# A graph layer on one core: in each step the transposes of the probabilities go behind the score matmul and the projections

## The chip, the cores and the metric

The kernel runs on one core of a Trainium2 chip. The metric is the device time of one execution in microseconds (us). TensorE is called PE here, VectorE DVE, ScalarE ACT, GpSimd POOL and SyncE SP. SP only issues transfers. Each engine executes its own instruction stream in the order in which it is written, and engines wait for each other through semaphores.

## What is computed

The input is 16 graphs of 512 nodes with 512 features each, and a 512x512 adjacency matrix for each graph. Two layers follow each other, each with a residual and a layer norm:

```
q, k, v = heads(x @ Wq.T), heads(x @ Wk.T), heads(x @ Wv.T)      # 16 heads of 32
a = einsum('bhnd,bhmd->bhnm', q, k) * scale + (adj + adj)
a = where(any(a != 0, axis=-1), a, -inf);  p = where(isnan(softmax(a)), 0, softmax(a))
x = layernorm(x + (p @ v, heads joined) @ Wo.T)
top1 = argmax(x.mean(axis=1) @ router_w + router_b);  W = expert_w[top1]     # one of 4
out = adj @ (x @ W);  mean, var = statistics of out over all graphs of the same expert
x = layernorm(x + relu((out - mean) * rsqrt(var + eps) * gamma + beta))
```

## The kernel before, in words

**Steps.** Attention is cut into steps. A step is one head and one tile of 128 query rows. Four heads are a group and are worked on together. A unit `u` is one group and one row tile, so it has 4 steps (`HG = 4`). A graph has 16 units and 64 steps, and 16 graphs give 1024 steps. A step handles a 128x512 tile of scores.

**One tile's way through the engines.** PE multiplies q and k into a PSUM bank (`pe_scores`, L325). There are two score banks. DVE adds the adjacency and finds the row extreme (`dve_logits`, L468). POOL folds the tile to a row sum that tells whether a row is all zero (L617, L619, L624). ACT takes the exponential (`act_exp_step`, L407). DVE normalises (L494). PE transposes the tile with four 128x128 transposes into one of two banks, `t_bank` (`pe_turn`, L334). ACT copies this bank to `pt` (L446). After two units PE multiplies `pt` with v (`pe_pv`, L347): 32 matmuls, once per 8 steps. This is called the PV block below, and there are 8 per graph.

**A software pipeline.** In step r the engines work on different tiles: PE transposes tile r and makes the scores of tile r + 12 (`LEAD = 12`). ACT copies the transposed tile r and takes the exponential of tile r + 10 (`EXP_LEAD = 10`). DVE does the logits of tile r + 12 and the normalisation of tile r + 6.

**Projections as filler.** All dense matmuls of the two layers are tasks: "V", "K", "Q" make v, k, q of this graph, and "Q+", "K+" those of the next. "O-", "sum-", "route-", "X-", "S-", "M-" finish the graph before: output projection, column means, router, transposes of x, x times expert, adjacency product. A task has four chunks, and most chunks are three 128x512 matmuls (L252 to L254), since each float32 operand is split into a high and a low part. A fixed list (`TASKS`, `HALF_SLOTS`) spreads the chunks over the 64 steps: in most steps one or two. Tasks alternate between two banks, `p_bank`. The first chunk of a task waits until the earlier task on its bank has been read out.

**Who reads a task out.** ACT and DVE have their part of a task in the step in which its last chunk stands. ACT does it behind the copy to `pt` and behind the exponential of that step. For Q, K, X and S tasks ACT copies the high part, and then DVE subtracts it to form the low part (L500, L501). For V and M tasks ACT reads alone, for O tasks DVE reads alone. These places matter here:

- V, task 3 has its last chunk in step 7, the step before the first PV block of a graph. The PV block also waits for v to be complete (`act_v`).
- X tasks 0 and 1 stand in step 32, and K+ task 0 begins in step 33 on the bank of X task 0.
- S task 0 ends in step 37, and S task 1 begins in step 38 with data from X task 1, on the bank that K and S tasks used; its predecessor there is S task 0.
- S task 1 ends in step 40, and S task 2 begins in step 41 on the same bank.
- In steps 24 to 27 ACT splits the next graph's transposed input, one quarter each step, ahead of that step's copy to `pt`. DVE makes the low part. Q+ task 0 in step 28 waits for all quarters.

**ACT's order in a step** (`act_slot`): wait for the transposes of tile r, copy them to `pt`, exponential of tile r + 10, then the tasks of the step. **DVE's order** (`dve_slot`): logits of tile r + 12, normalisation, then the tasks of the step.

**PV's waits** are these lines of `pe_pv`; the first asks for the copies of all transposes up to the end of the unit:

```
wait(eng, act_pt, b, STEPS, 4 * u + 4)
wait(eng, dve_ot, b, PAIRS, pair - 1)
wait(eng, act_v, b, NT, NT)
```

The first graph has no work of a graph before it (no O-, sum-, route-, X-, S-, M- tasks). The last has no Q+ and K+ tasks. The 14 graphs between have all tasks. Behind the 16 graphs one more round finishes the last graph without any attention steps, and a final loop normalises all graphs (from L1007 on DVE).

Of the kernel before, what the change touches and what calls it, by code (L numbers as in the profile page):

```python
# [54 lines left out]
def build_gnn_layers(nc, x, xT, adj, adjT, wqT, wkT, wvT, woT, router_w, router_b, experts, gammaT, betaT, out):  # L55
# [16 lines left out]
    with ctx:  # L72
# [89 lines left out]
        def wait(eng, s, b, per, more):  # L162

            if isinstance(b, int):
                if per * b + more > 0:
                    eng.wait_ge(s, per * b + more)
            else:
                assert per * 2 + more > 0
                eng.wait_ge(s, b * per + more)
                if eng.engine == mybir.EngineType.SP:  # L170
                    settle(eng)
# [59 lines left out]
        def wait_bank(eng, b, task, kind, kind_before):  # L231
            t, back = bank_user_before(task, kind, kind_before)
            s, per, more = done_by(b, t)
            wait(eng, s, b, per, more - per * back)
# [10 lines left out]
        def plan(u, kind):  # L245

            return [[c for c in step_chunks[HG * u + j] if present(c[0][0], *kind)] for j in range(HG)]


        def three_pass(eng, bank, lhs, rhs, kt, last):  # L250

            eng.matmul(bank, lhs(0), rhs(0), start=(kt == 0), stop=False)  # L252
            eng.matmul(bank, lhs(0), rhs(1), start=False, stop=False)  # L253
            return eng.matmul(bank, lhs(1), rhs(0), start=False, stop=last)  # L254

        def pe_chunk(eng, b, task, c, kind, kind_before):

            name, i = task
            bank = p_bank[bank_of[task]]
            if c == 0:  # L260
                wait_bank(eng, b, task, kind, kind_before)
            if name[0] in "QK":
                which = "QK".index(name[0])
                g = i if not name.endswith("+") else GROUPS + i
                if c == 0:
                    first = sum(t[0] == ("Q+", "K+")[which] for t in AHEAD)
                    wait(eng, (ld_qw, ld_kw)[which], b, GROUPS * 16, (g + 1 - first) * 16)
                    if i == 0:
                        wait(eng, dve_xt, b, DT, 2 * DT)
                        wait(eng, act_xt, b, DT, 2 * DT)  # L270
                mm = three_pass(eng, bank[:, :], lambda h: qk_w[:, which, h, c, :], lambda h: xt[:, h, c, :],
                                c, c == DT - 1)
            elif name == "V":
                if c == 0 and i == 0:
                    wait(eng, ld_wv, b, 16, 16)
                mm = three_pass(eng, bank[:, :], lambda h: xt[:, h, c, i * P:(i + 1) * P],
                                lambda h: slot_a[:, h, c, :], c, c == DT - 1)
            elif name == "O-":
                if c == 0 and i == 0:
                    wait(eng, ld_wo, b, 16, 0)  # L280
                    wait(eng, dve_ot, b, PAIRS, 0)
                mm = three_pass(eng, bank[:, :], lambda h: ot[:, h, c, i * P:(i + 1) * P],
                                lambda h: slot_b[:, h, c, :], c, c == DT - 1)
            elif name == "sum-":
                if c == 0:
                    wait(eng, dve_x1, b, NT, 0)
                for t in range(NT):
                    mm = eng.matmul(bank[:, c:c + 1], x1[:, t, c * P:(c + 1) * P], ones[:, :],  # L288
                                    start=(t == 0), stop=(t == NT - 1))
            elif name == "route-":  # L290
                if c == 0:
                    wait(eng, dve_mean, b, 1, 0)
                mm = eng.matmul(bank[:, 0:E], xmean[:, c:c + 1].to_broadcast([P, P]), rw[:, c, :],
                                start=(c == 0), stop=(c == DT - 1))
            elif name == "X-":
                mm = eng.transpose(bank[:, c * P:(c + 1) * P], x1[:, i, c * P:(c + 1) * P], ident[:, :])
            elif name == "S-":
                if c == 0:
                    wait(eng, dve_lo["X"], b, NT, i + 1 - NT)
                    if i == 0:  # L300
                        wait(eng, ld_ex, b, 16, 0)
                mm = three_pass(eng, bank[:, :], lambda h: x1t[:, i % 2, h, c, :], lambda h: slot_a[:, h, c, :],
                                c, c == DT - 1)
            else:
                if c == 0 and i == 0:
                    wait(eng, dve_lo["S"], b, NT, 0)
                    wait(eng, pool_at, b, NT, 0)
                mm = three_pass(eng, bank[:, :], lambda h: sup[:, h, c, i * P:(i + 1) * P],
                                lambda h: slot_b[:, h, c, :], c, c == NT - 1)
            if c == 3:  # L310
                mm.then_inc(pe[name.rstrip("+-")], 1)
# [5 lines left out]
        def pe_scores(eng, b, r):  # L317

            u, j = divmod(r, HG)
            g, t = divmod(u, NT)  # L320
            if j == 0 and t == 0:
                wait_stacked(eng, 0, b, g)
                wait_stacked(eng, 1, b, g)
            wait(eng, dve_logit, b, STEPS, r - 1)
            eng.matmul(s_bank[r % 2][:, :], q_stack[:, g % 2, j, t * P:(t + 1) * P], k_stack[:, g % 2, j, :],  # L325
                       start=True, stop=True).then_inc(pe["score"], 1)

        def pe_turn(eng, b, r):

            u, j = divmod(r, HG)  # L330
            wait(eng, dve_norm, b, STEPS, r + 1)
            wait(eng, act_pt, b, STEPS, r - 1)
            for m in range(NT):
                mm = eng.transpose(t_bank[r % 2][:, m * P:(m + 1) * P],  # L334
                                   att[:, u % 4, j, m * P:(m + 1) * P], ident[:, :])
            mm.then_inc(pe["turn"], 1)

        def pe_pv(eng, b, u):

            pair, g = u // 2, u // NT  # L340
# [3 lines that stand above are left out]
            for m in range(NT):  # L344
                for j in range(HG):
                    head = g * HG + j
                    mm = eng.matmul(o_bank[pair % 2][j * HD:(j + 1) * HD, 0:2 * P],  # L347
                                    v[:, m, head * HD:(head + 1) * HD], pt[:, j, m, :],
                                    start=(m == 0), stop=(m == NT - 1), tile_position=(0, j * HD))
            mm.then_inc(pe["pv"], 1)  # L350

        def pe_slot(eng, b, u, kind, kind_before):
            attends, has_next = kind[2], kind[1]
            work = plan(u, kind) if u >= 0 else [[]] * HG
            for j in range(HG):
                r = HG * u + j
                if attends and r >= 0:
                    pe_turn(eng, b, r)
                if (attends and r + LEAD < STEPS) or (has_next and r + LEAD >= STEPS):
                    pe_scores(eng, b, r + LEAD)  # L360
                for task, c in work[j]:
                    pe_chunk(eng, b, task, c, kind, kind_before)
            if attends and u >= 0 and u % 2 == 1:
                pe_pv(eng, b, u)

# [712 lines left out]
```

## Time and profile before

| | |
|---|---|
| time, median of 3 runs | 2675.96 us (2672.56 to 2677.76) |
| profiled execution: its own time | 2680.46 us |
| span in the profile | 2678.7 us |
| PE busy | 2336.3 us, 87% |
| DVE busy | 2075.9 us, 77% |
| ACT busy | 1715.0 us, 64% |
| POOL busy | 1784.4 us, 67% |
| mean granted clock of PE | 0.904 of full speed |

The times are of unprofiled runs. The profile is of one separate execution. Busy time of PE is modelled: matmuls overlap, so that a start-to-start distance is shorter than the printed duration (three 128x512 matmuls start 0.23 us apart and are printed with 0.39 us each).

### The profile page before, as it was taken

What the parts mean: (1) busy time and instruction counts of PE and PEld (TensorE: products, weight loads), DVE (VectorE), ACT (ScalarE), POOL (GpSimd) and SP (SyncE); (2) the same over time, 40 slices, a digit from 0 to 9 for tenths busy, and PEclk for the clock granted to TensorE, in tenths of its full rate; (3) what the DMA queues carried; (4) which work ended last, traced back from release to release, by engine and by line L of the source; (5) the groups of instructions that cost most, each with busy time, mean ns of one, the idle gap of its engine ahead of it and who ended that gap; (6) DMA issues with size and microseconds to landing.
All of it is one profiled execution on the core that took longest, in us unless ns stands there. A gap on an engine that the chain in (4) does not pass through costs nothing.

```text
span 2678.7 us, 50494 instructions
## 1 busy us (share of the span) xinstructions
PE 2336.3 (87%) x14976; PEld 1826.5 (68%) x14976; DVE 2075.9 (77%) x5107; ACT 1715.0 (64%) x3838; POOL 1784.4 (67%) x3148
## 2 busy tenths in 40 slices
PE   2678999999999999999999999999999999986433
PEld 2456777777777777777777777777777777765332
DVE  2687878887887878788888878787887887872588
ACT  0467676777767676767677676777776776762232
POOL 0678786877777777868777777777786877770000
PEclk7789898999989898989999898989998999987755
DMA  6577464555555565646555555656464555523597
GB/s 213 185 233 228 147 216 147 172 175 159 173 176 177 153 204 149 214 143 190 158 162 173 177 177 154 204 154 205 151 212 136 173 167 175 148 81 122 189 332 248
DMA packets 215897, 478.88 MB, mean 179 GB/s; under 512 B 41424, under 2 KB 49616, under 8 KB 208720
## 3 DMA queue, kind: packets, MB, share of 16 engines
q1 hardware_dynamic: 215632, 475.71, 56.7%
q8 instruction: 121, 1.98, 0.3%
q14 instruction: 144, 1.18, 0.1%
HBM read 274.23 MB, written 67.11 MB: 127 GB/s over the span
## 4 chain that ended last, share of the span: by engine, by line
PE 68%; DVE 13%; ACT 5%; issue 5%; POOL 4%; SPq 3%; DMA 2%; DVEq 0%; POOLq 0%; ACTq 0%
PE t_bank L334 14%; PE p_bank L252 12%; PE p_bank L254 11%; PE p_bank L253 11%; PE o_bank L347 9%; PE s_bank L325 7%; PE p_bank L288 3%; SPq L646 2%; DVE att L468 2%; ACT att L407 2%; POOL fold L617 2%; DVE ln_raw L1004 2%; DVE att L494 1%; POOL fold L619 1%; DVE xt L500 1%
## 5 line engine op out<-in xcount | busy, mean ns | idle before, releaser
L617 POOL TENSOR_TENSOR fold<-att 128x256 f32<-128x256 f32 x1024 | 821.3, 802 | 471.3 <-DVE nmax L468 366.9
L446 ACT ACTIVATE pt<-t_bank 128x512 f32<-128x512 f32 x1024 | 611.5, 597 | 561.1 <-PE t_bank L334 550.1
L468 DVE CUSTOM_DVE_ANT_0 att<-s_bank,adj_t 128x512 f32<-128x512 f32 x1024 | 699.0, 683 | 297.2 <-PE s_bank L325 295.4
L407 ACT ACTIVATE att<-att,nmax 128x512 f32<-128x512 f32 x1024 | 736.0, 719 | 85.5 <-POOL fold L617 63.2
L494 DVE TENSOR_SCALAR att<-att,small 128x512 f32<-128x512 f32 x1024 | 689.1, 673 | 9.3
L334 PE MATMUL t_bank<-ident,att 128*128 128x128 f32 x4096 | 644.4, 281 | 6.5 <-ACT pt L446 6.3
L334 PEld LDWEIGHTS t_bank<-ident,att 128*128 128x128 f32 x4096 | 515.7, 145 | 186.4 <-issue 48.5
L619 POOL TENSOR_TENSOR fold<-fold 128x128 f32<-128x128 f32 x1024 | 523.2, 511 | 80.3
L325 PE MATMUL s_bank<-k_stack,q_stack 128*128 128x512 f32 x1024 | 504.2, 493 | 80.4 <-DVE nmax L468 80.0
L624 POOL TENSOR_TENSOR fold<-fold 128x64 f32<-128x64 f32 x1024 | 357.9, 349 | 80.2
L347 PE MATMUL o_bank<-pt,v 128*32 128x256 f32 x4096 | 276.1, 415 | 28.0 <-ACT pt L446 15.6
L325 PEld LDWEIGHTS s_bank<-k_stack,q_stack 128*128 128x128 f32 x1024 | 201.3, 197 | 93.5 <-DVE nmax L468 90.9
L252 PE MATMUL p_bank<-xt,qk_w 128*128 128x512 f32 x492 | 207.4, 422 | 35.0 <-DVE xt L500 23.8
L347 PEld LDWEIGHTS o_bank<-pt,v 128*32 128x32 f32 x4096 | 130.6, 117 | 147.7 <-issue 50.7
L254 PE MATMUL p_bank<-xt,qk_w 128*128 128x512 f32 x492 | 204.5, 416 | 0.0
L253 PE MATMUL p_bank<-xt,qk_w 128*128 128x512 f32 x492 | 204.1, 415 | 0.0
L407 ACT ACTIVATION_READ_ACCUMULATOR att<-att,nmax 128x1 f32 x1024 | 198.2, 194 | 0.0
L252 PEld LDWEIGHTS p_bank<-xt,qk_w 128*128 128x128 f32 x492 | 101.0, 205 | 52.7 <-issue 28.4
L252 PE MATMUL p_bank<-slot_a,x1t 128*128 128x512 f32 x256 | 104.3, 408 | 29.3 <-DVE sup L500 21.1
L476 DVE TENSOR_REDUCE small<-fold 128x4 f32<-128x256 f32 x256 | 106.3, 415 | 27.5 <-POOL fold L624 26.8
L376 ACT ACTIVATE qk_t<-p_bank 128x512 fp32r<-128x512 f32 x128 | 75.7, 591 | 76.7 <-DMA q_stack<-qk_t 37.0
L631 POOL TENSOR_TENSOR slot_b<-stage,slot_b 128x512 fp32r<-128x512 f32 x64 | 83.6, 1327 | 55.8 <-ACT slot_b L431 55.8
(150 smaller groups left out, 3591.5 us busy)
## 6 DMA issues: line engine op xcount, KB each, us to landing
q_stack<-qk_t SPq DMA_DIRECT2D x1024, 64.0 KB, 2.0
k_stack<-qk_t SPq DMA_DIRECT2D x1024, 64.0 KB, 2.0
qk_w<-qk_split SPq DMA_DIRECT2D x123, 512.0 KB, 4.3
slot_a<-vo_split SPq DMA_DIRECT2D x16, 2048.0 KB, 8.2
slot_b<-vo_split SPq DMA_DIRECT2D x16, 2048.0 KB, 9.5
slot_a<-expert_split SPq DMA_DIRECT2D x16, 2048.0 KB, 8.1
stage<-in_xT SPq DMA_DIRECT2D x16, 1024.0 KB, 14.9
adj_t<-in_adj SPq DMA_DIRECT2D x64, 256.0 KB, 3.1
```

Source lines behind the costliest of these rows:

```text
L252: eng.matmul(bank, lhs(0), rhs(0), start=(kt == 0), stop=False)
L253: eng.matmul(bank, lhs(0), rhs(1), start=False, stop=False)
L254: return eng.matmul(bank, lhs(1), rhs(0), start=False, stop=last)
L325: eng.matmul(s_bank[r % 2][:, :], q_stack[:, g % 2, j, t * P:(t + 1) * P], k_stack[:, g % 2, j, :], start=True, stop=True).then_inc(pe["sc ...
L334: mm = eng.transpose(t_bank[r % 2][:, m * P:(m + 1) * P], att[:, u % 4, j, m * P:(m + 1) * P], ident[:, :])
L347: mm = eng.matmul(o_bank[pair % 2][j * HD:(j + 1) * HD, 0:2 * P], v[:, m, head * HD:(head + 1) * HD], pt[:, j, m, :], start=(m == 0), stop ...
L407: eng.activation(att[:, u % 4, j, :], att[:, u % 4, j, :], ACT.Exp, bias=nmax[:, u % 4, j:j + 1], scale=-1.0, accum_out=rsum[:, u % 4, j:j ...
L446: eng.activation(pt[:, j, :, (u % 2) * P:(u % 2 + 1) * P], t_bank[r % 2][:, :].rearrange("p (m n) -> p m n", m=NT), ACT.Copy).then_inc(act ...
L468: eng.tensor_tensor_reduce(out=att[:, u % 4, j, :], in0=s_bank[r % 2][:, :], in1=adj_t[:, t, :], scale=-2.0, scalar=3.0e38, op0=ALU.add, o ...
L494: eng.tensor_scalar(att[:, u % 4, j, :], att[:, u % 4, j, :], rinv[:, j:j + 1], live[:, j:j + 1], ALU.mult, ALU.mult).then_inc(dve_norm, 1)
L617: eng.tensor_tensor(fold1[:, :], a[:, 0:256], a[:, 256:512], ALU.add).then_inc(pool_fold1, 1)
L619: eng.tensor_tensor(fold1[:, 0:P], fold1[:, 0:P], fold1[:, P:2 * P], ALU.add).then_inc(pool_halved, 1)
```

## The change

In each step of `pe_slot` the call of `pe_turn` moves from the front to the end, behind the score matmul and behind the step's chunks. The PV block, which follows every eighth step, stays where it is, and so comes directly behind the transposes. Nothing else is changed: the same instructions with the same waits are issued, and the other engines keep their order.

```diff
             for j in range(HG):
                 r = HG * u + j
-                if attends and r >= 0:
-                    pe_turn(eng, b, r)
                 if (attends and r + LEAD < STEPS) or (has_next and r + LEAD >= STEPS):
                     pe_scores(eng, b, r + LEAD)
                 for task, c in work[j]:
                     pe_chunk(eng, b, task, c, kind, kind_before)
+                if attends and r >= 0:
+                    pe_turn(eng, b, r)
             if attends and u >= 0 and u % 2 == 1:
                 pe_pv(eng, b, u)
```

## Rows read from the trace of the kernel before

**Rows 1.** The page: busy time by engine, and the chain by engine.
```profile
PE 2336.3 (87%) x14976; PEld 1826.5 (68%) x14976; DVE 2075.9 (77%) x5107; ACT 1715.0 (64%) x3838; POOL 1784.4 (67%) x3148
...
PE 68%; DVE 13%; ACT 5%; issue 5%; POOL 4%; SPq 3%; DMA 2%; DVEq 0%; POOLq 0%; ACTq 0%
```

**Rows 2.** Waits, whole span: who waits for whom, us in total, times, longest.
```profile
ACT pt L446 <- PE t_bank L334: 550.1, 492, 6.9
...
DVE att L468 <- PE s_bank L325: 295.4, 248, 3.8
...
PE s_bank L325 <- DVE nmax L468: 80.0, 35, 29.2
```

**Rows 3.** Windows: one graph in the middle; us, busy by engine, clock.
```profile
1137.00:1287.00 150.00, 143.57 (x946) 112.60 (x939) 120.63 (x302) 105.51 (x239) 112.43 (x198) 0.94 0.56 170
```

**Rows 4.** Timeline before a graph's first PV block: start, us, engine, work, [idle before].
```profile
1132.33 0.60 PE L334 MATMUL t_bank<-ident,att 128*128 128x128 f32 x4
...
1132.96 0.60 ACT L446 ACTIVATE pt<-t_bank 128x512 f32<-128x512 f32 x1 [0.71 <-PE t_bank L334]
...
1133.45 0.71 ACT L407 ACTIVATE att<-att,nmax 128x512 f32<-128x512 f32 x1
...
1134.59 0.60 ACT L382 ACTIVATE v<-p_bank 128x512 f32<-128x512 f32 x1 [0.33 <-PE p_bank L254]
1135.33 1.93 PE L347 MATMUL o_bank<-pt,v 128*32 128x256 f32 x32 [0.78 <-ACT v L382]
```

**Rows 5.** Timeline at an ordinary PV block, step 15.
```profile
1149.55 0.60 PE L334 MATMUL t_bank<-ident,att 128*128 128x128 f32 x4
...
1150.68 0.40 PE L254 MATMUL p_bank<-slot_b,ot 128*128 128x512 f32 x1
...
1151.01 1.93 PE L347 MATMUL o_bank<-pt,v 128*32 128x256 f32 x32
```

**Rows 6.** Timeline in the first graph, whose steps are short.
```profile
128.80 3.35 PE L347 MATMUL o_bank<-pt,v 128*32 128x256 f32 x32 [2.66 <-ACT pt L446]
```

**Rows 7.** Timeline, steps 32 and 33: X transposes, exponential, first K+ chunk.
```profile
1197.92 1.04 PE L296 MATMUL p_bank<-ident,x 128*128 128x128 f32 x8
...
1198.99 0.19 ACT L407 ACTIVATION_READ_ACCUMULATOR att<-att,nmax 128x1 f32 x1
...
1200.45 0.50 PE L252 MATMUL p_bank<-xt,qk_w 128*128 128x512 f32 x1 [0.83 <-DVE x1t L500]
```

**Rows 8.** Timeline, steps 37 and 38: from S task 0 to S task 1.
```profile
1208.82 0.60 PE L334 MATMUL t_bank<-ident,att 128*128 128x128 f32 x4
...
1210.31 0.68 DVE L500 TENSOR_TENSOR sup<-p_bank,sup 128x512 fp32r<-128x512 f32 x1
...
1211.04 0.50 PE L252 MATMUL p_bank<-slot_a,x1t 128*128 128x512 f32 x1 [0.95 <-DVE sup L500]
```

**Rows 9.** Timeline, steps 40 and 41: from S task 1 to S task 2.
```profile
1217.28 0.60 PE L334 MATMUL t_bank<-ident,att 128*128 128x128 f32 x4
1217.48 0.60 ACT L394 ACTIVATE sup<-p_bank 128x512 fp32r<-128x512 f32 x1 [0.32 <-PE p_bank L254]
...
1218.85 0.50 PE L252 MATMUL p_bank<-slot_a,x1t 128*128 128x512 f32 x1 [0.31 <-DVE sup L500]
```

**Rows 10.** Timeline, steps 25 to 28: the split of the next input.
```profile
1170.67 0.60 PE L334 MATMUL t_bank<-ident,att 128*128 128x128 f32 x4
...
1172.73 0.60 PE L334 MATMUL t_bank<-ident,att 128*128 128x128 f32 x4
...
1173.37 0.60 ACT L446 ACTIVATE pt<-t_bank 128x512 f32<-128x512 f32 x1 [0.24 <-PE t_bank L334]
...
1176.18 0.61 ACT L440 ACTIVATE xt<-stage 128x512 fp32r<-128x512 f32 x1
...
1177.26 0.94 DVE L500 TENSOR_TENSOR xt<-stage,xt 128x512 fp32r<-128x512 f32 x1
...
1178.46 0.76 PE L252 MATMUL p_bank<-xt,qk_w 128*128 128x512 f32 x1 [1.65 <-DVE xt L500]
```

**Rows 11.** Windows behind these waits; the column after POOL is the granted clock.
```profile
1177.00:1184.00 7.00, 5.54 (x15) 4.48 (x16) 6.96 (x16) 5.13 (x11) 5.00 (x10) 0.51 0.41 103
...
1199.00:1202.00 3.00, 2.17 (x12) 1.53 (x11) 2.58 (x7) 3.00 (x9) 1.97 (x4) 1.00 0.93 399
```

## The prediction, written before the changed kernel was run

> **What bounds the kernel now.** I read the page first. PE is busy 87% of the span, and the chain of work that ended last runs on PE for 68% and on DVE for 13% [rows 1]. Then the list of waits. The two largest are ACT waiting for the transposes, 550.1 us in 492 waits, and DVE waiting for scores, 295.4 us; the other way round PE waited for DVE's logits for only 80.0 us, of which one wait was 29.2 us [rows 2]. So PE sets the pace and the others wait for it. Third, the windows: a graph in the middle takes 150 us and PE is busy for 143.57 us of them [rows 3]. A microsecond that PE loses inside a graph is therefore lost for good, unless it falls where PE waits for ACT or DVE anyway. Such places are few: the waits of rows 4 and 7 to 10.
>
> **What the change does to PE's stream.** Transposes T, scores S and chunks C come in the order T S C T S C before, and S C T S C T after. In the middle of a run of steps this is the same cycle; the transposes are only one place later with regard to the scores. Nothing is added or removed, no transfer or queue is touched. The normalised tile that T reads was made six steps earlier, so T has nothing new to wait for. S finds its bank as free as before. The steps between two events cost nothing. What changes is what T's position sets off: ACT starts its step with a wait for T, and so everything that ACT does in a step, the task read-outs too, moves from beside S and C to behind them.
>
> **Part 1: ordinary PV blocks.** PV needs the copy of the transposes of its last step. Before, S and C lie between T and PV. At step 15, T starts at 1149.55, the last chunk matmul at 1150.68, and PV at 1151.01 without a wait [rows 5]. After, PV is next behind T. From T's start to ACT's copy is 0.63 us (1132.33 to 1132.96), the copy takes 0.60, and a read-out on ACT ends 0.14 us before PV starts (1134.59 + 0.60 to 1135.33) [rows 4]: together 1.37 us. Chunk end to PV was 0.10 us (a third matmul is done 0.23 after its start: 1150.91 to 1151.01). So PV comes 1.27 us later behind the last chunk, less the 0.36 us of T that no longer stand ahead of that chunk: +0.91 us. Seven of the eight PV blocks of a graph are of this kind: 6.4 us. The lower end is 0, if ACT's copy were hidden; nothing stands between T and PV to hide it. The upper end is the 2.66 us that PV waited for the same copy in the first graph, where a step holds little but T and S [rows 6]. I take 0.91, since its pieces are all from a full graph.
>
> **Part 2: the first PV block of a graph.** It also needs V task 3, whose read-out stands on ACT behind copy and exponential. The row has 0.95 us from V's last chunk (1134.38) to PV. After, it is 0.63 + 0.49 (copy start to exponential start) + 0.90 (exponential with its accumulator read) + 0.60 + 0.14 = 2.76 us [rows 4], so +1.81 less 0.36: +1.45 us.
>
> **Part 3: tasks that wait for the task just before.** Here ACT's high part and DVE's low part of one task stand between two chunks. After the change, from the last chunk's end: 0.63 + 0.49 + 0.90 on ACT behind T, 0.60 high part, about 0.70 low part, 0.14 to PE = 3.46 us. Before:
> - S task 0 to S task 1: 1208.82 to 1211.04 = 2.22 us, with a PE wait of 0.95 [rows 8]. +1.24.
> - S task 1 to S task 2: 1217.28 to 1218.85 = 1.57 us, because ACT was free at once (1217.48) [rows 9]. +1.89.
> - X to K+: 2.53 us from the first X transpose (1197.92) to K+ [rows 7]. After: 0.88 for the eight X transposes, then 3.46, less the 0.68 of T32 (at half clock) that no longer stands ahead: 3.66. +1.1.
>
> The sum is 4.2 us per graph. The lower end is 0, where DVE and not the read-out was late; the upper end is the full 3.46 thrice, 10.4. PE's own work in between is in both numbers. I stay at 4.2: in two of the three the idle time of PE is put down to just this low part.
>
> **Part 4: the split of the next input, steps 25 to 28.** ACT is a chain of its own here. Its copy of tile 25 now waits for a T that starts at 1172.37 instead of 1170.67 (behind the chunks), 1.70 later. Of that, ACT's own idle 0.24 goes, and DVE's low part began 0.47 after the high part was ready (1176.18 + 0.61 to 1177.26): +1.0 us left on Q+ [rows 10]. Bounds: 0 and 1.7.
>
> **Part 5: DVE held by the late high parts.** DVE stands still until ACT has written the high part of its task, now up to 3.4 us after the task's last chunk; logits of the next tile are queued behind that low part. They end some 4.15 us after the chunk. The score matmul that needs this bank comes three steps later, 3.8 us after the chunk if the two steps are of 1.37 and 2.06 us, 4.5 if both are long. Short by 0.45 or not at all. For 12 such tasks a graph the bounds are 0 and 5.4 us. I take 2.0, since some of the 12 are in Part 3 already or have a PV block behind them.
>
> **Sum.** 6.4 + 1.45 + 4.2 + 1.0 + 2.0 = 15.0 us for each of 14 full graphs: 210. The last graph has no parts 4 and 5: 12. The first has few tasks and its PV blocks wait already: 3. Together 225 us, no gain anywhere to set against it, except that S follows PV directly (below). The profiled execution took 2680.5 us, span 2678.7: 2905 after. The median of the runs is 4.5 us lower: 2901.
>
> **Rivals.**
> - *Only the PV blocks count* (22%). DVE is busy 120.63 of 150 us [rows 3], and a PE that stands at PV lets DVE and ACT catch up, so that parts 3 to 5 hit engines with more slack. For: DVE's work trails its scores in the busy stretches. Against: the S waits are set by latency, not by a backlog. Then 15 x 7.9 = 118, and 2794.
> - *The clock falls at the new waits* (20%). PE's two waits of 1.57 and 1.65 us before Q+ are followed by 7 us at a granted clock of 0.51 [rows 10, 11], that is the lower of the two levels, 1.2 GHz. Waits of 0.62 and 0.83 us near 1200 left it at 1.00 [rows 7, 11]. New waits of some 2.2 us at V, K+ and S lie between these. If two of them per graph start such a stretch, each costs half of 7 us: 14 x 2 x 3.4 = 95, and 2996. The Trainium skill, in "TensorE: Matmul & The Clock Gate", Part 4, says that transposes don't count as PE activity in the way of matmuls; the change puts them right ahead of the waits, and by that page this rival is likelier than I make it. The trace neither shows it nor excludes it: there transposes run at a granted clock of 1.00, but always between matmuls.
> - *Scores behind PV decide, and it gets faster* (4%). During a PV block DVE runs out of scores (its waits for them are 295.4 us [rows 2]). The change lets S follow PV without T between, 0.41 us sooner, 128 times: 52 us, and 2624. This would decide if DVE's logits were what the end hangs on. Against: PE waited for them only 80 us, DVE catches up within a step, and the price of part 1 is paid ahead of each of these gains.
> - *Nothing moves* (4%). The cycle is the same, and waits swap places: within 0.2% of 2676. It needs PE slack of 1 us at each PV block, which rows 5 don't show.
>
> **From these to the numbers.** The forecast has 50%: 2901. The range reaches from just under the PV-only case to just over the clock case, 2785 to 3005. About 0.2% is what a measurement of this kernel can tell from no change. Faster 0.04, same 0.04, slower 0.92.
>
> **What would show it.** In the changed profile the wait of PE's `o_bank` for ACT's `pt` grows from a few us to about 7 x 0.95 us a graph, 100 us or more in the whole, each close to 1 us. The first PV of a graph waits 2 us or more for v. The waits of PE for S and X low parts become 2 us each. The time from one graph to the next grows from 150 to some 165 us, and PE's share falls to about 80%. The waits of DVE and POOL for PE grow. If the wait at PV is missing, or the graph's period is still near 150 us, part 1 is wrong. If a period is above 170 us and the granted clock below 0.88, the clock rival holds. If PE waits for logits (L468) after Q and K tasks, part 5 is larger than I took it.

## The result and the profile after

The changed kernel takes 2937.68 us (median of 4 runs, 2935.32 to 2939.50) against 2674.26 for the kernel before beside it: ratio 1.0983, 95% interval 1.0964 to 1.1002. That is 263 us more. I had forecast 2901 (225 more) within 2785 to 3005, and slower with 0.92. The direction and the range held, and so did the mechanism of the two largest terms; the size was 37 us short.

The page of the changed kernel. The first line answers to the busy times in [rows 1], the second to the chain there:

```profile
PE 2399.5 (82%) x14976; PEld 1854.9 (63%) x14976; DVE 2058.0 (70%) x5107; ACT 1695.4 (58%) x3838; POOL 1785.6 (61%) x3148
...
PE 59%; DVE 17%; ACT 10%; issue 7%; POOL 2%; SPq 2%; DMA 1%; DVEq 0%; ACTq 0%; POOLq 0%
```

The counts of instructions are those of before, so no engine has more to do. PE's busy time is still 63 us longer; some of its matmuls are printed longer at half clock, as shown below. Its busy share falls from 87% to 82%, while the share of ACT and DVE in the chain grows by 9 points. This is how added latency looks, as against added work.

The waits of the changed kernel, whole span, with the columns of [rows 2]:

```profile
ACT pt L446 <- PE t_bank L334: 956.7, 684, 6.0
...
PE s_bank L325 <- DVE nmax L468: 120.2, 75, 29.1
...
PE o_bank L347 <- ACT pt L446: 83.4, 112, 2.2
...
PE p_bank L252 <- DVE sup L500: 63.5, 33, 2.2
...
PE p_bank L252 <- DVE x1t L500: 33.1, 14, 2.4
...
PE o_bank L347 <- ACT v L382: 31.4, 16, 2.0
...
PE p_bank L293 <- DVE small L524: 14.4, 16, 1.6
```

The same waits of the kernel before, as far as [rows 2] does not have them:

```profile
PE p_bank L252 <- DVE sup L500: 22.5, 33, 1.5
...
PE o_bank L347 <- ACT pt L446: 15.6, 10, 2.9
PE o_bank L347 <- ACT v L382: 12.5, 16, 0.8
...
PE p_bank L252 <- DVE x1t L500: 11.2, 14, 0.8
...
PE p_bank L293 <- DVE small L524: 6.3, 16, 0.8
```

The number of waits is the thing to see. PV waited for the copy 10 times, now 112 times: every ordinary PV block of all 16 graphs, 7 x 16. The low-part waits are as many as before (33 and 14) and nearly three times as long in total.

**The time from one graph to the next** is read from the first PV block of two graphs in a row, on PE's timeline. In the kernel before, the block after that of [rows 4] (1135.33) starts at 1282.10, so a graph takes 146.8 us:

```profile
1282.10 1.93 PE L347 MATMUL o_bank<-pt,v 128*32 128x256 f32 x32 [0.78 <-ACT v L382]
```

After, the first PV row below to the second is 164.1 us. Over 14 graphs the means are 146.5 and 163.8 us, 17.3 us apart. The row above the first is that of the transposes right ahead of it.

```profile
1240.12 0.60 PE L334 MATMUL t_bank<-ident,att 128*128 128x128 f32 x4
...
1242.68 1.93 PE L347 MATMUL o_bank<-pt,v 128*32 128x256 f32 x32 [1.97 <-ACT v L382]
...
1406.76 1.94 PE L347 MATMUL o_bank<-pt,v 128*32 128x256 f32 x32 [1.96 <-ACT v L382]
```

**An ordinary PV block after**, step 15, which answers to [rows 5]:

```profile
1258.30 0.60 PE L334 MATMUL t_bank<-ident,att 128*128 128x128 f32 x4
...
1258.93 0.60 ACT L446 ACTIVATE pt<-t_bank 128x512 f32<-128x512 f32 x1 [0.41 <-PE t_bank L334]
...
1259.58 1.93 PE L347 MATMUL o_bank<-pt,v 128*32 128x256 f32 x32 [0.69 <-ACT pt L446]
```

From the transposes' start to PV it is 1.28 us, of which the transposes issue for 0.36. So PE stands still for 0.92 us. The row says 0.69, because PE's ends are modelled: the transposes are printed with 0.60 us. A wait behind transposes is 0.24 us longer than its row. A wait behind a chunk is longer than its row too, by 0.17 us, since the last matmul is printed with 0.40 and takes 0.23. Before, 0.10 us lay between chunk and PV [rows 5], so the change adds 0.82 us.

**The waits for low parts after**, which answer to [rows 7, 8, 9]:

```profile
1313.60 0.79 PE L252 MATMUL p_bank<-xt,qk_w 128*128 128x512 f32 x1 [2.36 <-DVE x1t L500]
...
1326.75 0.56 PE L252 MATMUL p_bank<-slot_a,x1t 128*128 128x512 f32 x1 [2.03 <-DVE sup L500]
...
1338.60 0.50 PE L252 MATMUL p_bank<-slot_a,x1t 128*128 128x512 f32 x1 [1.93 <-DVE sup L500]
```

Before they were 0.83, 0.95 and 0.31 us. The first of these matmuls is printed with 0.79 us against 0.50 in [rows 7]: PE's granted clock has just fallen. The windows show it; the third number from the right is the granted clock, 0.5 of full speed being 1.2 GHz:

```profile
1310.00:1313.00 3.00, 1.24 (x10) 0.92 (x8) 0.63 (x4) 1.96 (x5) 1.74 (x3) 1.00 0.64 273
1313.00:1317.00 4.00, 3.40 (x11) 2.71 (x11) 3.25 (x8) 1.10 (x3) 1.57 (x3) 0.57 0.00 0
1322.00:1326.00 4.00, 2.73 (x16) 2.06 (x14) 3.56 (x8) 3.65 (x9) 3.84 (x5) 1.00 0.42 101
1326.00:1330.00 4.00, 3.25 (x10) 2.69 (x11) 2.41 (x8) 0.95 (x2) 3.35 (x7) 0.63 0.45 109
```

The kernel before has no half-clock stretch in these two places. Its granted clock was 0.904 over 2678.7 us, the changed kernel's 0.897 over 2937.7: 257 us and 303 us of full clock withheld (span times the missing share), 45 us more.

**Steps 25 to 28 after**, which answer to [rows 10]:

```profile
1283.96 0.50 PE L325 MATMUL s_bank<-k_stack,q_stack 128*128 128x512 f32 x1 [0.54 <-DVE nmax L468]
...
1287.97 0.80 PE L325 MATMUL s_bank<-k_stack,q_stack 128*128 128x512 f32 x1 [3.08 <-DVE nmax L468]
1290.12 0.76 PE L252 MATMUL p_bank<-xt,qk_w 128*128 128x512 f32 x1 [1.36 <-DVE xt L500]
```

DVE makes the low part of the input ahead of its logits, and it stood still 2.36 us for ACT's high part:

```profile
1282.58 0.71 DVE L500 TENSOR_TENSOR xt<-stage,xt 128x512 fp32r<-128x512 f32 x1 [2.36 <-ACT xt L440]
```

PE stands still for 0.54 + 3.08 + 1.36 = 4.98 us. Before, it waited 1.65 us for xt [rows 10] and once for logits, which this row of the kernel before shows; together 3.22:

```profile
1176.31 0.50 PE L325 MATMUL s_bank<-k_stack,q_stack 128*128 128x512 f32 x1 [1.57 <-DVE nmax L468]
```

### The profile page after: what moved, and what is told of

Read it like the earlier page. It is cut to its first block, busy times and chain, and to the rows that moved or that the text cites. A ratio compares the mean times of both kernels' runs of the same rounds, so it can differ in the third digit from the quotient of the medians.

```text
span 2937.7 us, 50494 instructions
## 1 busy us (share of the span) xinstructions
PE 2399.5 (82%) x14976; PEld 1854.9 (63%) x14976; DVE 2058.0 (70%) x5107; ACT 1695.4 (58%) x3838; POOL 1785.6 (61%) x3148
## 4 chain that ended last, share of the span: by engine, by line
PE 59%; DVE 17%; ACT 10%; issue 7%; POOL 2%; SPq 2%; DMA 1%; DVEq 0%; ACTq 0%; POOLq 0%
PE t_bank L334 11%; PE p_bank L252 10%; PE p_bank L254 10%; PE p_bank L253 10%; PE o_bank L347 9%; PE s_bank L325 7%; ACT att L407 4%; DVE att L468 4%; ACT pt L446 3%; DVE att L494 3%; DVE ln_raw L1004 2%; PE p_bank L288 1%; SPq L646 1%; POOL fold L617 1%; DVE ln_raw L518 1%
## 5 line engine op out<-in xcount | busy, mean ns | idle before, releaser
L407 ACT ACTIVATE att<-att,nmax 128x512 f32<-128x512 f32 x1024 | 734.1, 717 | 20.9 <-POOL fold L617 17.3
L494 DVE TENSOR_SCALAR att<-att,small 128x512 f32<-128x512 f32 x1024 | 666.9, 652 | 9.3
L334 PEld LDWEIGHTS t_bank<-ident,att 128*128 128x128 f32 x4096 | 535.1, 147 | 137.6 <-issue 13.3
L325 PE MATMUL s_bank<-k_stack,q_stack 128*128 128x512 f32 x1024 | 514.9, 504 | 123.2 <-DVE nmax L468 120.2
L619 POOL TENSOR_TENSOR fold<-fold 128x128 f32<-128x128 f32 x1024 | 533.8, 521 | 80.3
L624 POOL TENSOR_TENSOR fold<-fold 128x64 f32<-128x64 f32 x1024 | 351.9, 344 | 80.3
L347 PE MATMUL o_bank<-pt,v 128*32 128x256 f32 x4096 | 276.9, 416 | 114.8 <-ACT pt L446 83.4
L325 PEld LDWEIGHTS s_bank<-k_stack,q_stack 128*128 128x128 f32 x1024 | 201.8, 197 | 215.7 <-DVE nmax L468 150.2
L252 PE MATMUL p_bank<-xt,qk_w 128*128 128x512 f32 x492 | 211.6, 430 | 55.5 <-DVE x1t L500 33.1
L253 PE MATMUL p_bank<-xt,qk_w 128*128 128x512 f32 x492 | 207.2, 421 | 0.0
L254 PE MATMUL p_bank<-xt,qk_w 128*128 128x512 f32 x492 | 206.4, 419 | 0.0
L252 PEld LDWEIGHTS p_bank<-xt,qk_w 128*128 128x128 f32 x492 | 101.4, 206 | 74.6 <-DVE x1t L500 37.5
L501 DVE SCALAR_TENSOR_TENSOR qk_t<-p_bank,qk_t 128x512 fp32r<-128x512 f32 x64 | 44.3, 692 | 119.5 <-ACT qk_t L376 119.5
L254 PEld LDWEIGHTS p_bank<-xt,qk_w 128*128 128x128 f32 x492 | 100.9, 205 | 24.5
```

Source lines behind the costliest of these rows:

```text
L334: mm = eng.transpose(t_bank[r % 2][:, m * P:(m + 1) * P], att[:, u % 4, j, m * P:(m + 1) * P], ident[:, :])
L407: eng.activation(att[:, u % 4, j, :], att[:, u % 4, j, :], ACT.Exp, bias=nmax[:, u % 4, j:j + 1], scale=-1.0, accum_out=rsum[:, u % 4, j:j ...
L494: eng.tensor_scalar(att[:, u % 4, j, :], att[:, u % 4, j, :], rinv[:, j:j + 1], live[:, j:j + 1], ALU.mult, ALU.mult).then_inc(dve_norm, 1)
L619: eng.tensor_tensor(fold1[:, 0:P], fold1[:, 0:P], fold1[:, P:2 * P], ALU.add).then_inc(pool_halved, 1)
```

## The experiments

All times are medians, and each ratio is to the kernel before, run beside it. Differences between experiments are differences of these medians. The kernel before itself read 2673 to 2676 us beside them, so such a difference is good to a few us. Where nothing else is said, an edit is shown against the changed kernel. The question was how the 263 us split between the PV blocks and the read-outs, and whether anything is left when both are gone.

### e2: only the PV part

```diff
+                last = (j == 3 and u % 2 == 1)
+                if attends and r >= 0 and not last:
+                    pe_turn(eng, b, r)
                 ...
-                if attends and r >= 0:
+                if attends and r >= 0 and last:
                     pe_turn(eng, b, r)
```

Expected: 

> The mirror of e1: the kernel before, and only in the step before each PV block the transposes stand last. Theory A: 2674 + 118 = 2792 us, each ordinary PV block waits 0.69 us by the profile, the first of a graph some 1.97 us, and the waits for low parts stay at their size before (0.3 to 1.0 us). Rival B (engines absorb what stands alone): under 2735 us. If e1 and e2 add up to the whole change (their distances from the kernel before sum to 263 us), the costs are separate.

Measured: 2784.02 us, ratio 1.0393 (1.0367 to 1.0419), 109 us more. Its waits of PE:

```profile
PE o_bank L347 <- ACT pt L449: 85.5, 112, 3.1
...
PE o_bank L347 <- ACT v L385: 31.4, 16, 2.0
PE p_bank L252 <- DVE sup L503: 23.1, 33, 1.5
...
PE p_bank L252 <- DVE x1t L503: 11.0, 14, 0.8
```

One eighth of the transposes moved makes two fifths of the loss. The PV waits are those of the whole change, the low-part waits those of the kernel before. PE's waits for logits grew a little, from 80.0 to 90.1 us. My 118 was too high by some 14 us: it took the hidden 0.24 us as new, but idle that no row shows stood ahead of PV before, 0.10 us at an ordinary block and 0.17 at the first of a graph. Rival B of the expectation, that engines absorb such waits, falls.

### e1: the change without its PV part

The same edit with `last = not (j == 3 and u % 2 == 1)`.

Expected: 

> As the changed kernel, but in the step before each PV block the transposes stand first again. Theory A (three separate costs: the copy that PV waits for, ACT's read-outs behind the transposes, DVE held by them): the PV waits go and nothing else does. In the changed profile PE waits 83.4 + 31.4 us there, 15.6 + 12.5 before, and 128 blocks hide another 0.24 us each in the modelled end of the transposes: 118 us. So 2938 - 118 = 2820 us, and the waits for x1t and sup low parts stay at some 2 us each. Rival B (PV waits give the others time to catch up): without them the DVE waits grow and over half of the 118 comes back, above 2880 us. Rival C (the clock): the granted clock rises by more than 0.01.

Measured: 2880.28 us, ratio 1.0750 (1.0728 to 1.0772): 57 us gained back, not 118. But this is not a clean removal, which I had not seen. Transposes that stand last in one step and first in the next follow each other at once. ACT then has two copies and an exponential in a row, and PV waits for it still:

```profile
PE o_bank L347 <- ACT pt L449: 39.2, 67, 1.9
...
PE o_bank L347 <- ACT v L385: 17.6, 16, 1.1
```

These are 56.8 us against 114.8 in the changed kernel. That accounts for the 57 us as far as waits go, and the run says nothing for rival B. Its granted clock was 0.893, no higher than that of the changed kernel.

### e3: ACT's read-outs ahead of its copy

```diff
+                for task, c in work[j]:
+                    if c == 3:
+                        act_task(eng, b, task, kind)
                 if attends and r >= 0:
                     wait(eng, pe["turn"], b, STEPS, r + 1)
                 ...
-                for task, c in work[j]:
-                    if c == 3:
-                        act_task(eng, b, task, kind)
```

Expected: 

> The changed kernel, and on ACT the read-outs of a step's tasks stand ahead of the copy to pt and the exponential, so that they no longer wait for the transposes. Theory A: parts 3 and 5 go and the v read-out before a graph's first PV too; what is left are 128 copies at 0.92 us, 118 us: 2792 us, with PE's waits for x1t and sup back under 1 us. Rival B (exponentials are then late instead, since ACT now waits for chunks): the logits and normalisation come later, waits of the transposes for normalised tiles appear, and it stays above 2880 us.

Measured: 2782.63 us, ratio 1.0398 (1.0379 to 1.0418): 155 us of the 263 gone without a touch to PE's order. Its waits:

```profile
PE o_bank L347 <- ACT pt L449: 108.1, 128, 2.6
...
PE p_bank L252 <- DVE sup L500: 23.1, 33, 1.5
```

The wait for x1t has shrunk from 33.1 to 3.7 us. The v read-out is ahead of the copy now, so all 128 PV blocks wait for the copy. PE's waits for logits stay long: 112.8 us, against 120.2 in the changed kernel and 80.0 in the kernel before. The granted clock is 0.914, so 239 us of full clock are withheld, 64 fewer than in the changed kernel. Shorter waits make some 90 of the 155 us, and the clock can make the rest.

### e4: the PV block one step later

```diff
                 for task, c in work[j]:
                     pe_chunk(eng, b, task, c, kind, kind_before)
+                if j == 0 and u > 0 and u % 2 == 0 and attends:
+                    pe_pv(eng, b, u - 1)
+                if j == 0 and u == 0 and kind[0] and attends:
+                    pe_pv(eng, b - 1, UNITS - 1)
                 if attends and r >= 0:
                     pe_turn(eng, b, r)
-            if attends and u >= 0 and u % 2 == 1:
+            if attends and u == UNITS - 1 and not has_next:
                 pe_pv(eng, b, u)
```

Expected: 

> The changed kernel, and the PV block is issued one step later, between the chunks and the transposes of the next step, so that a score matmul and chunks cover the copy. Theory A: the ordinary PV waits go (7 x 0.92 us x 16 = 103 us) and most of the first one's 1.4 us: about 2825 us, the same as e1. Rival B: as in e1, above 2880 us. If it is far below e1, the place of the PV block matters beyond the wait (scores for DVE come directly behind the transposes).

Measured: 2840.72 us, ratio 1.0610 (1.0590 to 1.0630), 97 us gained; expected were 113. The waits for the copy are no longer among PE's larger ones, and v is waited for only 5.4 us in 16 times. Those for low parts are unchanged at 63.9 and 33.1 us, and those for logits grew from 120.2 to 150.2:

```profile
PE s_bank L325 <- DVE nmax L472: 150.2, 124, 29.1
...
PE p_bank L252 <- DVE sup L504: 63.9, 33, 2.2
...
PE p_bank L252 <- DVE x1t L504: 33.1, 14, 2.4
```

So here a part of the PV gain does come back, as waits for DVE that late read-outs hold up; the router's wait grew too, from 14.4 to 23.3 us. That is the only sign of part 5 of the prediction, and it needs the PV waits gone. The granted clock rose to 0.905, 34 us less withheld, though the low-part waits are as long as in the changed kernel.

### e5: both remedies

Expected: 

> The changed kernel with both remedies: the PV block one step later, and ACT's read-outs ahead of its copy to pt. If the change costs by these two latencies alone, PE's stream is the cycle of the kernel before again, and the time is that of the kernel before: 2660 to 2685 us. A few us below it are possible, since e4 shows PV waiting for v only 0.34 us instead of 0.78, and the scores follow directly behind some PV blocks. Rival (the transposes behind scores and chunks cost by themselves, through exponentials that ACT starts later): above 2700 us, with PE waits for DVE's logits.

Measured: 2678.89 us over 10 runs, ratio 1.0013 (1.0001 to 1.0024). All transposes still stand last in their step, and some 3, at most 6, of the 263 us are left on balance. Its waits of PE show that this is a balance and not an absence:

```profile
PE s_bank L325 <- DVE nmax L472: 126.3, 64, 29.1
...
PE p_bank L252 <- DVE sup L504: 16.2, 18, 1.5
```

The waits for logits are 46 us longer than in the kernel before (80.0 in 35 times). In a middle graph they are the 0.5 and 3.08 us of part 4, which neither remedy touches. Against them stand waits that the kernel before had and e5 has not: 27 us at PV, 11 for x1t and 6 for sup. So the 46 us that the order still costs are made up by 44 us of old waits. What the order costs by itself can't be read from this ratio. The run that would tell, the kernel before with both remedies, was not made. The few us below the kernel before that I thought possible did not come.

### e10 and e11: the read-outs split in two

As e3, with `if c == 3 and task[0] in ("X-", "S-")` moved ahead for e10, and the others (`not in`) for e11.

Expected of e10: 

> The changed kernel, and on ACT only the read-outs of X and S tasks stand ahead of the copy to pt; all transposes still stand last. It takes away part 3 alone. In the profiles the waits for x1t and sup grew by 60 us in 14 graphs, 64 in 15, and 41 us more of granted clock were lost in stretches right behind them: theory with the clock 2938 - 64 - 41 = 2833 us, and the granted clock rises from 0.897 to about 0.91. Without the clock: 2874 us, clock near 0.90.

Expected of e11: 

> The complement of e10: on ACT only the read-outs of Q, K, V and M tasks stand ahead of the copy. It takes away part 5, the router's wait, and v ahead of the first PV block, and leaves part 3. e3 took away both and gained 155 us; with 105 for part 3 this gains 50: 2888 us. By the waits: logits 32 us, router 8, v 1.4 x 16 = 23, together 63: 2875 us. The granted clock stays near 0.897. If it gains over 90 us, part 5 is the larger one.

Measured: e10 2836.88 us, ratio 1.0634 (1.0610 to 1.0657), so 101 us gained; e11 2886.26, ratio 1.0811 (1.0791 to 1.0831), 51 us. Together 152, against the 155 of e3. By the ratios, each to the kernel before beside it, the shares are 93 and 46 us against 156. The profiles settle it better: over the 14 middle graphs the time from graph to graph falls by 6.8 us in e10, 3.4 in e11 and 10.3 in e3. So the two are separate. In e10's waits of PE the one for x1t is down from 33.1 to 4.3 us, and the one for sup is shorter than its 63.5:

```profile
PE p_bank L252 <- DVE sup L503: 39.7, 33, 2.2
```

These two make 53 of the 101 us. The granted clock rises from 0.897 to 0.913: 247 us of full clock withheld over a span of 2834.9 us, against 303, 56 us less. Removing waits of 2 us returned more than the waits. The same holds for e11, where I had expected the clock to stay near 0.897. It rose to 0.905, 29 us less withheld, while the waits for sup and x1t stayed at 61.2 and 33.1 us and all of PE's waits together shrank by some 18. In one-microsecond windows from 1200 to 1500 us, e10 has two stretches at half clock per graph, as the kernel before has, where the changed kernel has three or four.

### e6: scores, transposes, chunks

```diff
                     pe_scores(eng, b, r + LEAD)
+                if attends and r >= 0:
+                    pe_turn(eng, b, r)
                 for task, c in work[j]:
                     pe_chunk(eng, b, task, c, kind, kind_before)
-                if attends and r >= 0:
-                    pe_turn(eng, b, r)
```

Expected: 

> Half of the change: the score matmul ahead of the transposes, the chunks behind them. Theory: what costs is that the transposes stand behind the chunks. Here the low-part waits stay as before, and a PV block has only chunks to cover the copy: with one chunk 0.36 + 0.70 us against the 1.37 us that the copy needs, short by 0.31 in some five blocks of a graph, nothing in those with two chunks. 2675 + 16 x 5 x 0.31 = 2700 us. Rival (scores first feeds DVE earlier behind a PV block and gains): below 2670 us.

Measured: 2675.89 us over 10 runs, ratio 1.0016 (1.0006 to 1.0026). The chunks, not the score matmul, were the part that must not stand ahead. This may be a balance too: the granted clock is 0.915, some 30 us less withheld than in the kernel before, and the waits for logits are 102 us against 80. My 25 us for uncovered copies were a miss. At step 15 of this kernel PV starts 1.29 us behind the transposes' start (1017.44 to 1018.73), held up by the copy, and transposes, chunk and the usual start gap of 0.10 take 1.16. Short by 0.13, not 0.31: 1.37 was pieced together from rows of different blocks. The rival, scores early and so faster, falls.

### e7, e8, e9: the transposes last in some steps only

The edit of e2 with other conditions for `last`: steps with no read-out and no PV block (e7), steps 32, 37 and 40 (e8), the other read-out steps (e9).

Expected of e7: 

> The kernel before, and the transposes stand last only in those steps in which ACT reads no task out, which are not ahead of a PV block and not among the four that split the next input (steps 24 to 27). Theory A: nothing that PE needs stands behind them, so within 8 us of 2675. Rival (the order costs by itself in every step, by later exponentials): some 4 us per graph and more, above 2720 us.

Expected of e8: 

> The kernel before, and the transposes stand last only in steps 32, 37 and 40, behind which K+ task 0 and S tasks 1 and 2 wait for the low part made just before. Theory A with the clock: 4.2 us of waits per graph, 15 graphs, 63 us, and in the profile of the changed kernel 41 us more of granted clock are lost in 14 graphs, in stretches that begin right behind these waits: 2675 + 63 + 41 = 2779 us, granted clock near 0.90. Theory A without the clock: 2738 us at 0.907 or more.

Expected of e9: 

> The kernel before, and the transposes stand last only in steps 1, 3, 5, 10, 18, 29, 35, 38, 41, 43, 46, 48, 50, 53, 58 and 60: ACT reads a task out there, but no chunk waits for it at once. This is part 5 alone, DVE held by the late high part and the next logits late. By the estimate 2.0 us per full graph: 2703 us; its bounds were 0 and 5.4 us per graph (2675 to 2751). In the profile PE's waits for logits (L325 on L468) grow from 80 us by about the same amount. Rival (these read-outs have slack): under 2685 us and no such waits.

Measured: e7 2735.40 us (ratio 1.0227, 1.0199 to 1.0254), e8 2710.03 (1.0114, 1.0074 to 1.0153), e9 2732.55 (1.0218, 1.0191 to 1.0245). All three missed. e7 should have cost nothing and cost 59 us. That is the number of its rival, that the order costs by itself in every step; e5, where every step has this order, is against that rival. The profile of e7 shows the fault of e1 again:

```profile
PE o_bank L347 <- ACT pt L449: 36.3, 54, 2.6
...
PE p_bank L252 <- DVE sup L503: 33.7, 33, 1.8
```

PV waits for the copy, though it has scores and chunks ahead of it, since the step before pushed its own transposes next to it. Where the order changes from step to step, ACT gets its copies in pairs and is late at the step behind. So e7 and e9 don't measure the steps that I named, and I read no split from them. In e8 the three waits are 1.93, 1.50 and 1.50 us (0.83, 0.95 and 0.31 before): about two thirds of the growth in the whole change. The waits for sup and x1t grew by 41 us in all and the time by 34, with a granted clock of 0.910. So the theory with the clock (2779 us) fails there: behind the wait of 1.93 us half clock followed in 1 of 14 graphs. The clean split is e3, e10 and e11, where all transposes stand last.

### e12: step 7 alone, scores behind the chunks

The kernel before with `pe_scores` moved behind the chunk loop where `attends and r % 64 == 7`.

Expected: 

> The kernel before, and in step 7 of each graph alone the score matmul stands behind the chunks, so that it covers 0.31 of the 0.78 us that the first PV block waits for v: 16 x 0.31 = 5 us, 2671 us if nothing else moves. Rival (the scores for DVE come late and it loses as much): 2676 us or more.

Measured: 2676.13 us over 12 runs, ratio 1.0011 (0.9995 to 1.0026). No gain of 5 us. The wait for v did fall, from 12.5 to 8.7 us; where the rest of the time went was not looked into. No version ran faster than the kernel before.

## Why the prediction was right, and where its size was off

**The cycle costs nothing by itself: right for ordinary steps.** In e5 all transposes stand last, and a middle graph has no wait of PE beyond those of steps 26 to 28 and the old ones for sup and the router. The ratio of 1.0013 alone would not show it, since the cost of part 4 stays in e5 and the remedies took old waits away.

**Part 1, ordinary PV blocks, +0.91 us each: right, a little too large.** From the transposes' start to PV it is 1.28 us and not 1.37, so each block costs 0.82 more than before, and 112 of 112 blocks wait. With part 2 the prediction has 118 us (15 x 7.9), and by the rows it is 5.7 + 1.25, that is 7.0 a graph. Alone it measures 109 (e2), which holds 10 us of waits for logits; taken out of the change it measures 97 (e4).

**Part 2, v ahead of the first PV, +1.45: right, a little too large.** The transposes start at 1240.12 and PV at 1242.68, 2.56 us, of which the transposes take 0.36. PE stands still for 2.20 us, against 0.95 before [rows 4]: +1.25.

**Part 3, waits for low parts, 4.2 us per graph: right as a wait, short as a cost.** The two waits grew by (63.5 - 22.5) + (33.1 - 11.2) = 62.9 us over 15 graphs, 4.2 each. That the sum fits so well is luck in part: the three waits grew by 1.53, 1.08 and 1.62 us where I had 1.1, 1.24 and 1.89. And e10 gets 101 us back, not 63. What I left out of the sum is the clock.

**The clock: this is the mis-sized step.** I had it as a rival with 20% and 3.4 us a stretch, two per graph, and took zero for the forecast. What is there lies between. In the changed kernel new half-clock stretches of 3 to 4 us stand behind the S wait in all of the 14 middle graphs and behind the K+ wait in 6 of them. In these 14 graphs 41 us more of full clock are withheld, 2.9 us per graph. My 3.4 came from the longer stretch of [rows 11]; a new stretch is 3 to 4 us long, and half of that is withheld. With 2.9 the sum would have been 17.9 per graph against 17.3 measured. With every part at its measured size it is 5.7 + 1.25 + 4.2 + 1.8 + 0.2 + 0.5 + 2.9 = 16.6, so 0.7 us stay unexplained. (5.7 is 7 x 0.82; 0.5 is the router's wait below.) One premise of the rival does not stand: it names a wait of 0.62 us near 1200, and the trace has none there, only the 0.83. That the half clock is caused by these waits rests on where the stretches begin and on e10; e4 and e11 also got clock back without touching them. The rule of the Trainium skill that I had set beside this rival (transposes don't count as PE activity in the way of matmuls, "TensorE: Matmul & The Clock Gate", Part 4) is not settled by it: in the second of these places chunks of matmuls and a wait of 2.03 us stand close together too, and no run here changes the transposes alone.

**Part 4, the split of the next input: 1.0 predicted, 1.8 measured** (4.98 - 3.22). The wait for xt got shorter (1.65 to 1.36). The loss lies in the score matmul one step earlier, which waits for logits that DVE does behind a late xt low part: 3.08 us. I had followed ACT's chain to Q+ and not DVE's queue to the scores. No experiment that puts all transposes last removes this wait: it is there in e3, e4, e5, e10 and e11 with the same 3.08 us.

**Part 5, DVE held by late high parts: 2.0 predicted, 0.2 measured.** Outside steps 26 to 28 the only new wait for logits in a graph is one of 0.2 us. DVE does stand still (DVE waits for qk_t, x1t and sup grew), but the PV waits and the low-part waits give it time to catch up. e4 shows the other half: with the PV waits gone, 30 us of waits for logits appear. In place of part 5 the router's wait was missing from my list: 6.3 to 14.4 us in 16 graphs, 0.5 each, from DVE held behind Q+ task 0.

**The base.** I wrote that a graph takes 150 us. That was the window I had asked for, not a period; it is 146.8. No term used it, but the forecast of "150 to 165" should read 147 to 162, and measured is 164.

**The rivals.** "Only the PV blocks count" would have been 2794; e2 is that kernel, 2784, and the change is not. "Scores behind PV decide" is out by the result and by e6, where the scores also follow PV directly and nothing is gained. "Nothing moves" is out by the result. "The clock falls" was partly true.

## What to carry to other kernels

In this software pipeline, moving one operation within a PE step left PE's own cycle as it was, but it moves the start of whatever engine begins its step with a wait for that operation, and of everything queued behind it there. Look for the places where PE needs something of that engine within one step (here the PV block and a handful of read-outs of a graph) and price each as latency minus the work in between. Where such a wait nears 2 us, a half-clock stretch behind it is a rival worth a price of its own; here it came behind some of them, at 1.7 us of full clock each. When a remedied kernel ties with the one before, try the remedy on the kernel before as well, or read whether old waits went with the new. To measure the parts of a reordering, move the waiting engine's work or the consumer in all steps alike; reversing the order in single steps makes pairs that cost by themselves.

## What the runs showed of the hardware

Half-clock stretches stood behind waits of PE far shorter than I had thought. In the changed kernel those of 2.36 us (1313.60) and 2.03 us (1326.75) were each followed by some 3 to 4 us at half clock. The waits of 1.93 us for the other S task (1338.60), of 1.97 us ahead of the first PV block and of 0.69 us ahead of the other PV blocks were not. In other kernels the first two of these were: in e2, the 1.96 us ahead of the first PV block in 9 of 14 middle graphs, and in e1, the 1.93 us for the other S task in 13 of 14. The first two lines are from e2, with PV printed at 3.61 us and not 1.93; the last is from e1, with the first matmul at 0.73 and not 0.50:

```profile
562.72 3.61 PE L347 MATMUL o_bank<-pt,v 128*32 128x256 f32 x32 [1.96 <-ACT v L385]
...
563.00:566.00 3.00, 3.00 (x32) 1.48 (x24) 0.00 (x0) 0.00 (x0) 0.00 (x0) 0.50 0.43 97
...
990.68 0.73 PE L252 MATMUL p_bank<-slot_a,x1t 128*128 128x512 f32 x1 [1.93 <-DVE sup L503]
```

Length alone doesn't decide it: the same K+ wait was followed by half clock in 6 of 14 graphs only, and one graph earlier it was as long and the matmul behind it was printed with its full-clock 0.50 us:

```profile
1150.86 0.50 PE L252 MATMUL p_bank<-xt,qk_w 128*128 128x512 f32 x1 [2.37 <-DVE x1t L500]
```

So neither the length of a wait nor its place decides it alone. What does was not tested.
